# Self attention's rotation in three separate VectorE steps, later pieces of the shared bank spaced anew, residual read first in its group

## The reference

```python
def _apply_rope(x, sin, cos):
    x1 = x[..., ::2]
    x2 = x[..., 1::2]
    r = jnp.stack([x1 * cos - x2 * sin, x1 * sin + x2 * cos], axis=-1)
    return r.reshape(x.shape)
...
q = (src @ Wq).reshape(Bb, Tt, H, DH).transpose(0, 2, 1, 3)
k = (src @ Wk_c @ Wk).reshape(Bb, Tt, H, DH).transpose(0, 2, 1, 3)
v = (src @ Wv_c @ Wv).reshape(Bb, Tt, H, DH).transpose(0, 2, 1, 3)
sin, cos = _rope_sincos(Tt, DH)
q = _apply_rope(q, sin, cos)
k = _apply_rope(k, sin, cos)
attn = jnp.einsum('bhqd,bhkd->bhqk', q, k) / np.sqrt(DH).astype(np.float32)
attn = jax.nn.softmax(attn, axis=-1)
sa = jnp.einsum('bhqk,bhkd->bhqd', attn, v)
sa = sa.transpose(0, 2, 1, 3).reshape(Bb, Tt, C) @ Wo
x = _rmsnorm(src + sa, norm1_w)
```

## Time and profile before

| what | value |
|---|---|
| time, median of 3 runs | 587.1 us (584.31, 587.1, 590.09) |
| time of the profiled execution | 585.65 us |
| its span, first to last instruction | 583.9 us |
| TensorE busy | 530.0 us (91% of the span) |
| VectorE busy | 283.0 us (48%) |
| ScalarE busy | 184.3 us (32%) |
| GpSimd busy | 126.1 us (22%) |
| cross stage's scores, from about | 203 us to 332 us |
| self attention, scores to last transposes back | 339.8 us to 417.9 us |

### The profile page before, as it was taken

How to read it: one execution, slowest core, us unless ns; L and a number is a source line. 1 busy time by engine, 2 the same in 40 slices (tenths; PEclk the granted TensorE clock), 3 DMA queues, 4 the chain that set the end, 5 groups by cost and what they waited for, 6 DMA issues and landing times. The chain is left out here.

```text
span 583.9 us, 9223 instructions
## 1 busy us (share of the span) xinstructions
PE 530.0 (91%) x3429; PEld 342.9 (59%) x3429; DVE 283.0 (48%) x660; ACT 184.3 (32%) x438; POOL 126.1 (22%) x146
## 2 busy tenths in 40 slices
PE   1989889899998879999999898989789999999995
PEld 1636565345556568887877677767535544444442
DVE  3436562112227455566576898786525222224242
ACT  1234231211113435555555545556522110000000
POOL 3012015011035352232332634431000000000000
PEclk9999989999999979999999999999979999999999
DMA  8989943479868595685552083000021000000000
GB/s 229 232 235 323 371 175 101 155 281 389 322 225 234 148 298 132 169 219 151 143 135 71 1 299 136 3 1 2 0 60 54 1 1 0 1 0 29 0 19 9
DMA packets 47087, 78.15 MB, mean 134 GB/s; under 512 B 6867, under 2 KB 36543, under 8 KB 46941
## 3 DMA queue, kind: packets, MB, share of 16 engines
q1 hardware_dynamic: 43841, 68.32, 38.1%
q0 software_dynamic: 3200, 9.22, 4.9%
HBM read 63.97 MB, written 12.13 MB: 130 GB/s over the span
## 5 line engine op out<-in xcount | busy, mean ns | idle before, releaser
L1386 PE MATMUL pb<-ring,big 128*128 128x512 f32 (+2 forms) x320 | 108.7, 593 | 2.3 <-DVE big L1337 1.2
L1386 PE MATMUL pb<-split 128*100 128x362 f32 (+2 forms) x320 | 78.6, 329 | 8.1 <-DVE nmx L1182 3.4
L1386 PEld LDWEIGHTS pb<-ring,big 128*128 128x128 f32 (+2 forms) x320 | 44.1, 166 | 59.4 <-issue 54.9
L1182 DVE TENSOR_REDUCE nmx<-pb 100x1 f32<-100x361 f32 x128 | 62.9, 527 | 29.3 <-PE pb L1386 28.8
L1386 PEld LDWEIGHTS pb<-split 128*100 128x100 f32 (+2 forms) x320 | 56.1, 183 | 18.3 <-issue 6.6
L858 ACT ACTIVATE big<-pb 121x400 f32<-121x400 f32 (+1 forms) x96 | 48.2, 504 | 24.8 <-PE pb L1386 22.5
L1358 DVE SCALAR_TENSOR_TENSOR ctxbuf<-pb,ctxbuf 128x256 f32<-128x256 f32 x48 | 23.2, 484 | 55.5 <-PE pb L1386 54.6
L1386 PE MATMUL pb<-big,arena 121*32 121x100 f32 (+3 forms) x1072 | 47.8, 263 | 1.5 <-ACT arena L708 1.2
L1386 PE MATMUL pb<-hT,ring 128*128 128x400 f32 x128 | 43.8, 501 | 0.5 <-DVE big L1337 0.5
L635 POOL TENSOR_TENSOR shift<-consts,nmx 100x400 fp32r<-100x400 f32 x32 | 28.2, 881 | 66.5 <-DVE nmx L1182 66.4
L1386 PE MATMUL pb<-hT,wgu 128*128 128x400 f32 (+2 forms) x108 | 38.7, 506 | 3.0 <-DVE big L1158 1.1
(11 more groups left out here) (242 smaller groups left out, 775.7 us busy)
## 6 DMA issues: line engine op xcount, KB each, us to landing
ring<-in_L_ffn_gate_up_proj SPq DMA_DIRECT2D x12, 1024.0 KB, 8.4
split<-kx_dram SPq DMA_DIRECT2D x64, 181.0 KB, 3.9
ring<-in_L_ffn_down_proj SPq DMA_DIRECT2D x12, 512.0 KB, 7.4
kx_dram<-split POOLq DMA_DIRECT2D x16, 362.0 KB, 5.1
ctxbuf<-in_L_ffn_gate_up_proj SPq DMA_DIRECT2D x4, 1024.0 KB, 9.6
ring<-in_L_ffn_W_experts SPq DMA_DIRECT2D x4, 1024.0 KB, 11.3
split<-qx_dram SPq DMA_DIRECT2D x64, 50.0 KB, 2.0
ctxbuf<-in_ctxT SPq DMA_DIRECT2D x6, 361.0 KB
```

Source lines behind the costliest of these rows:

```text
L1182: nc.vector.tensor_reduce(nmx[:, t % 4, q:q + 1], PB[SB[n % 3]][0:T, 0:CTX], AX.X, ALU.max, negate=True) \
L1386: return nc.tensor.matmul(o, l, r, start=start, stop=stop)
```

## The change

`rotate_begin` is split into `rotate_swap` and `rotate_sine`, each with its own table of places, and `rotate_end` is now `rotate_add`. The steps of one part so stand in up to three different quads or groups, and most swaps and additions are at other places than before. GpSimd's cosines and spreads are in another order. In the shared bank the piece Q(1,1) goes from group 1 to group 4 and most that follow move one group later. In VectorE's group n = 4b the read of Y (`d_residual`) now stands ahead of the group's maximum instead of behind its subtraction.

```diff
-LATE_SELF = {0: ("n", NB - 1, 0), 1: ("Q", 1, 1), 2: ("t", NB - 1, 0), 3: ("y", NB - 1, 0), 4: ("C", 1, 0), 5: ("K", 1, 0),
...
+LATE_SELF = {0: ("n", NB - 1, 0), 2: ("t", NB - 1, 0), 3: ("y", NB - 1, 0), 4: ("Q", 1, 1), 5: ("C", 1, 0), 6: ("K", 1, 0),
+             7: ("K", 1, 1), 8: ("V", 3, 0), 9: ("g", 3, 0), 10: ("V", 4, 0), 11: ("Y", 0, 0), 12: ("Q", 2, 0), 13: ("Q", 2, 1),
+             14: ("C", 2, 0), 15: ("Y", 1, 0), 16: ("K", 2, 0), 17: ("K", 2, 1), 18: ("V", 5, 0), 19: ("Y", 2, 0),
...
-ROTATE_BEGIN = [25, 27, 28, 30, NQUAD + 3, NQUAD + 8, NQUAD + 13, NQUAD + 17]
-ROTATE_END = [26, 28, 29, 31, NQUAD + 5, NQUAD + 10, NQUAD + 15, NQUAD + 19]
+
+ROTATE_SWAP = [24, 25, 26, 30, NQUAD + 5, NQUAD + 8, NQUAD + 14, NQUAD + 18]
+ROTATE_SINE = [24, 26, 27, 30, NQUAD + 6, NQUAD + 9, NQUAD + 15, NQUAD + 19]
+ROTATE_ADD = [26, 28, 29, NQUAD + 1, NQUAD + 7, NQUAD + 11, NQUAD + 17, NQUAD + 21]
...
                 for r in range(3):
-                    if t == ROTATE_BEGIN[r] + 2:
+                    if t == ROTATE_SWAP[r] + 2:
                         times_cos(r)
-                if t == 30:
+                if t == 29:
                     spread_queries(0)
+            times_cos(3)
             spread_queries(1)
-            times_cos(3)
-            times_cos(4)
             inverse_root("d", only=2)
             spread_queries(2)
+            times_cos(4)
+            spread_queries(3)
             times_cos(5)
-            spread_queries(3)
+            spread_queries(4)
             times_cos(6)
-            spread_queries(4)
             spread_queries(5)
             times_cos(7)
...
+                if b >= 3 and g == 0:
+                    d_residual(b - 3)
                 dve.wait_ge(s("d_s"), n + 1)
...
-                if b >= 3 and g == 0:
-                    d_residual(b - 3)
```

More of the change, by code:

```diff
@@ L1191, in rotated, with rotate_swap @@
                 return (qT if ROTATE[r][0] == "q" else krT), ROTATE[r][1]
-            def rotate_begin(r):
+            def rotate_swap(r):
                 t, g = rotated(r)
@@ L1197, in rotate_begin, with rotate_sine, rotate_add @@
                     dve.wait_ge(s("d_rot"), r - 1)
+                nc.vector.stream_shuffle(rot[:, r % 2], t[:, :, 2 * T * g:2 * T * (g + 1)], SWAP_PAIRS).then_inc(s("d_swap"), 1)
+            def rotate_sine(r):
+                dve.wait_ge(s("d_swap"), r + 1)
                 w4 = rot[:, r % 2].rearrange("p k (b t) -> p k b t", t=T)
                 sin = consts[:, cs["sin"]].unsqueeze(1).unsqueeze(1).to_broadcast([128, KT, 2, T])
-                nc.vector.stream_shuffle(rot[:, r % 2], t[:, :, 2 * T * g:2 * T * (g + 1)], SWAP_PAIRS).then_inc(s("d_swap"), 1)
-                dve.wait_ge(s("d_swap"), r + 1)
                 link(nc.vector.tensor_tensor(w4, w4, sin, ALU.mult))
-            def rotate_end(r):
+            def rotate_add(r):
                 t, g = rotated(r)
@@ L1211, in rotations @@
                 for r in range(len(ROTATE)):
-                    if t == ROTATE_END[r]:
-                        rotate_end(r)
+                    if t == ROTATE_ADD[r]:
+                        rotate_add(r)
                 for r in range(len(ROTATE)):
-                    if t == ROTATE_BEGIN[r]:
-                        rotate_begin(r)
+                    if t == ROTATE_SWAP[r]:
+                        rotate_swap(r)
+                    if t == ROTATE_SINE[r]:
+                        rotate_sine(r)
             for t in range(AHEAD):
```

## The result

The changed kernel takes 583.6 us (median of 20 runs, 580.19 to 588.09) where the kernel before now has 587.57 (20 runs). Two runs of the kernel before, 635.71 us here and 695.5 us beside e8 (mean clock 0.755 where the others have 0.96 to 0.98), are of a slower state and stand in no ratio. The ratio is 0.9931, with a 95% interval of 0.9912 to 0.995: 4.0 us faster, 0.7%, inside the one per cent that was forecast. The profiled execution took 584.23 us with a span of 582.4.

The account below looks back on a forecast made before the run. TensorE bounds these stages, with VectorE late at single points; 1.1 + 0 + 1.0 - 0.2 + 2.1 plus 0.3 gave 4.3 us. Subtracted from 585.65 and 587.1, the middle was 582.1 us, range 578 to 586.5.

Parts of the forecast that it names:

- A: End of the cross stage: maxima come earlier with swap and sine product moved; 1.1 us gained, bounds 0.3 to 1.9.
- B: Self attention groups 0 to 3: the 1.06 us wait before Q(1,1) goes, but Q(1,1) is only postponed; gain 0.
- C: Groups 4 to 7: the 1.2 us wait for a K half's copy shrinks, K(1,1) waiting 0.5; gain 1.0 us.
- D: Groups 8 to 11: VectorE arrives about 0.7 us late, g and V wait for copies; loss 0.2 us.
- E: Group 12: TensorE's wait for the read of Y falls from 0.95 to 0.35 us; gain 0.6.
- F: Group 16: the wait for the read of Y falls from 0.95 to 0.8 us; gain 0.15.
- G: Group 20: the wait for the read of Y falls from 1.43 to 1.05 us; gain 0.4.
- H: Group 24: nothing stands in the way of the read of Y, so its whole wait goes; gain 0.95 us.
- the rival in which the seams close: Sine products of groups 15 and 19 precede the spreads, or A's better bound holds: 6 to 7 us gained, 580; chance 0.27.
- VectorE did not become the bound: Rival: VectorE bounds groups 8 to 23, losing 0.3 to 0.5 us per batch; 1 us gained, 585; chance 0.09.
- the clock's low stretch behind self attention: Rival: TensorE's half-clock stretch there comes elsewhere or not at all, 2 to 3 us either way; chance 0.03.
- the slower rival: GpSimd's next instruction takes the port before a waiting VectorE step, costing 3.8 us instead of 1.75; 589.5 to 591; chance 0.03.

Follow-up runs that it names:

- e8: Changed kernel: spread 2 before last inverse root, four rotation steps one group later, part 3's addition in group 2, spread 0 behind last diagonal; 581.43 us, ratio 0.9855.
- e1: Kernel before with one edit, the read of Y ahead of its group's maximum; 583.89 us, ratio 0.9912, stretch 99.59 us.
- e2: Changed kernel with the read of Y put back behind the subtraction; ratio 1.0012 to the kernel before, stretch 105.23 us.
- e5: Changed kernel with four rotation steps (additions of parts 4 and 5, sine products of 6 and 7) one group later; stretch 97.87 us.
- e6: Changed kernel: spread 2 before last inverse root, four rotation steps one group later, part 3's addition in group 3, spread 0 behind quad 30's diagonal; ratio 0.9925.
- e7: Changed kernel with only spread 0 put back behind the diagonal of quad 30; stretch 102.15 us.
- e4: Changed kernel with GpSimd's spread 2 ahead of the last unit's inverse root instead of behind it; stretch 98.75 us.

## Why the prediction was right, and where its parts were not

The time, its sign and the main mechanism hold: 582.1 forecast and 583.6 measured, 4.3 us of gain forecast from the sum, 4.0 by the ratio and 4.57 in the stretch. (From 587.57, the kernel before's median over 20 runs, the 4.3 would give 583.3.) How the gain divides is another matter. By place, from TensorE's starts of the scores of every fourth group (a piece that changed places is added back: Q 0.78, V 0.51, K 0.44):

| place | before, us | after, us | pieces moved out (+) or in (-) | gain | forecast |
|---|---|---|---|---|---|
| A, n of batch 5 to scores 0 | 24.98 | 24.05 | | 0.93 | 1.1 |
| B, to y of batch 7 | 6.96 | 6.47 | +0.78 | -0.29 | 0 |
| C, to scores 8 | 10.96 | 10.83 | -0.27 | 0.40 | 1.0 |
| D, to scores 12 | 9.57 | 9.19 | +0.27 | 0.11 | -0.2 |
| E, to scores 16 | 10.44 | 10.11 | -0.34 | 0.67 | 0.6 |
| F, to scores 20 | 9.42 | 9.74 | -0.44 | 0.12 | 0.15 |
| G, to scores 24 | 9.52 | 8.02 | | 1.50 | 0.4 |
| H, to scores 28 | 9.03 | 8.01 | | 1.02 | 0.95 |
| behind, to the last Y | 12.95 | 12.84 | | 0.11 | in the 0.3 |

*The read of Y* (E to H) was the largest term, and e1 and e2 show that it is the cause. The formula for what is left of its wait, 0.25 plus the cosine's delay, gives 0.25 for group 12 (the prediction writes 0.35 there without a reason) and 0.8 for group 16; measured 0.33 and 0.91. Moving the held steps away (e5) took both to nothing.

*The moved steps and pieces* were priced too high. The prediction gives the read 2.1 us (E to H) and the rest 1.9 (A to D); by place it is 3.3 and 1.15. By e1 the read alone gives 4.24 and all the rest 0.33: there scores 12 to scores 28 take 34.27 us, 4.14 less than before, and in the changed kernel, piece for piece, 3.31 less. What the moved steps win in A to D they mostly lose at the seams (the places where one batch's groups end and the next begin), by standing held ahead of the read. The prediction had these holds right, but never asked what the read would be worth without them.

*Group 20 failed.* I had the sine product of group 19 meet spread 6 and leave 1.05 us; it was not held, and the whole 1.43 went. The cosine's delay itself came as said (spread 6 began 0.85 us behind the scores' end). I had named the small margin (0.2 to 0.6) as a reason for the rival in which the seams close. So that rival came true in one of two seams.

*Place C failed.* The step was "I reckon that K(1,1) waits 0.5 us". It still waits 1.16, and that is the 0.6 that C lacks. I had `ln_rows` of group 6 held by the end of spread 2 only; it was held by the cosine behind it as well, 1.96 us for the pair:

```profile
352.89 2.87 POOL L602 TENSOR_TENSOR ctxbuf<-tT,consts 128x1600 f32<-128x1600 f32 x1
355.71 1.04 POOL L610 TENSOR_TENSOR tT<-tT,consts 128x400 f32<-128x400 f32 x1
```

*Place A* was mis-sized for the same reason, a pair of 2.60 us (spread 0, then the diagonal) and a second wait of 1.42 instead of 1.1. The first wait, 0.46, was as forecast (0.5). *Place B*: no wait before the scores of group 2, 1.03 before y, as said. The first maximum was to start near 339.65 (the prediction's own terms, 341.11 less 1.6, give 339.51); it started at 344.18, in the time of before 339.93, only when its scores were there (they end at 344.08), and TensorE also waited 0.29 us before the transposes of group 1.

Places C and G missed by 0.6 and 1.1 us in opposite directions, so that the sum is better than its parts is luck. Of the other rivals: VectorE did not become the bound, no step of the changed kernel was held for over 3 us, and the clock's low stretch behind self attention stayed where it was (0.69 granted from 424 to 427 us, 0.50 before). The double hold of the slower rival is real, as e6 and e7 show; the changed kernel keeps clear of it only in part.

## What to carry to other kernels

When a bank is shared by pieces in turn, read out the last piece before starting the next group's work: the reader's wait for new input is free time for it, and here that alone was worth 4.2 of the 4.6 us. Before placing a VectorE step with two SBUF inputs, lay it beside GpSimd's list: here a step that met a reading GpSimd instruction mostly cost what was left of that instruction. Moving four steps one group later cost nothing in e5, but in e8 a step moved later met the next spread and cost TensorE 0.85 us. Judge a rearrangement by a fixed stretch of TensorE's timeline when the effect is near one per cent, and check each part alone, since two parts can change each other's worth: the moved rotation was worth -1.4 us with the read last and +0.3 with it first. And when a wait of TensorE grows, look at the clock behind it before putting the whole loss down to the wait (1.5 us of e2's, 1.3 of e6's).

## What the runs showed that I had not expected

A step of VectorE is not held by every GpSimd instruction that had already begun in the record. Where it starts 0.28 to 0.34 us after a spread's or a diagonal's start, it takes its usual 0.56 and the GpSimd instruction is longer instead, a spread 3.57 or 3.63 us for 2.87 and a diagonal 1.60 for 0.86; where it starts 0.48 us or more after, it is held to the end. The traces of e2 and e4 to e7 repeat it. e8 has one step that does not fit: the addition of part 2 began 0.15 us after a spread that followed a diagonal without a pause, and took 3.14 us. This is the pair of group 19 in the kernel after:

```profile
388.36 3.57 POOL L602 TENSOR_TENSOR ctxbuf<-tT,consts 128x1600 f32<-128x1600 f32 x1
```

The rule of the Trainium skill ("SBUF — State Buffer", section "Who interferes with whom") that whoever issues first has the shared pair for the whole instruction agrees with the held rows (2.31, 2.75); by the starts in the record alone it would have held this one too. Where instructions of GpSimd follow without a pause, the traces go both ways. A step was kept out through several of them, for 4.09 us in e6 and 4.38 in the kernel before; and in that same kernel one got in between two spreads (376.86, 1.07 us long) and one between a spread and a diagonal, which then took 1.18 us for 0.86:

```profile
333.57 1.21 DVE L1208 TENSOR_TENSOR ctxbuf<-ctxbuf 128x400 f32<-128x400 f32 x1
```

What decides this no run here tells.

And the clock fell in the middle of three kernels, each time when TensorE came back from a wait: of 2.90 us in e6 and e7 (0.56 and 0.67 granted over the next 3.6 us, 1.34 and 1.37 us lost on top of the wait) and of 2.00 us in e2 (0.60 over 3.43, 1.54 lost). Behind the wait of 1.42 us in the changed kernel it stayed at 1.00. Each is one trace, so how surely it falls isn't shown.
